# Attention row maxima over two PSUM banks at a time, with splits and sums moved to other engines

## The reference

```
b, s, d = x.shape                                   # 4, 512, 128; NH = 16 heads, DH = 8
qkv = x @ W_qkv.T + b_qkv
q, k, v = parts of qkv.reshape(b, s, 16, 24)
scores = einsum('bqhd,bkhd->bhqk', q, k) / sqrt(8)
attn = softmax(scores, axis=-1)
out = einsum('bhqk,bkhd->bqhd', attn, v).reshape(b, s, d)
return out @ W_out.T + b_out

x = x + 0.5 * ffn(layernorm(x))
x = x + attention(layernorm(x))
x = x + 0.5 * ffn(layernorm(x))
```

## Time and profile before

| | us |
|---|---|
| median of three runs | 1564.73 |
| the profiled execution | 1565.24 |
| its span | 1563.5 |
| attention steps alone on the chip | 708.8 to 902.4 of the span |
| PE busy | 1474.1 |
| DVE busy | 1308.9 |
| ACT busy | 1209.7 |
| POOL busy | 976.3 |

### The profile page before, as it was taken

One profiled execution on the slowest core, in us unless ns is written; L12 is line 12 of the kernel. 1 busy time (PEld: TensorE's weight loads), 2 busy tenths in 40 slices (PEclk: granted clock), 3 DMA queues, 4 the chain that ended last, 5 costly groups with the idle time before them and its releaser, 6 DMA issues. The chain is left out here.

```text
span 1563.5 us, 25918 instructions
## 1 busy us (share of the span) xinstructions
PE 1474.1 (94%) x7227; PEld 1101.0 (70%) x7227; DVE 1308.9 (84%) x3532; ACT 1209.7 (77%) x3587; POOL 976.3 (62%) x1719
## 2 busy tenths in 40 slices
PE   4898999999999999978988899999999999999997
PEld 3577778888888888743333347888888888888884
DVE  6989889988998877868898948988898889887884
ACT  3677888888888888737886687888888888888884
POOL 3477887777777776642332125777677767776665
PEclk8899999999999999979998999999999999999999
DMA  6144433333343235301211012233233233333321
GB/s 196 41 162 148 162 135 109 108 109 108 109 135 109 108 109 202 109 27 68 72 55 64 27 55 82 108 109 108 109 115 109 108 109 115 110 115 116 125 83 34
DMA packets 50838, 163.49 MB, mean 105 GB/s; under 512 B 3460, under 2 KB 26630, under 8 KB 34310
## 3 DMA queue, kind: packets, MB, share of 16 engines
q1 hardware_dynamic: 50694, 161.82, 29.8%
HBM read 136.64 MB, written 25.17 MB: 103 GB/s over the span
## 5 line engine op out<-in xcount | busy, mean ns | idle before, releaser
L989 ACT ACTIVATE vt<-bank,gate 128x128 f32<-128x128 f32 x1024 | 293.3, 372 | 169.1 <-PE bank L520 152.1
L1349 DVE SCALAR_TENSOR_TENSOR ot<-bank,gn,ot 128x128 f32<-128x128 f32 x1024 | 288.1, 344 | 82.7 <-ACT ot L1028 51.3
L1636 POOL TENSOR_TENSOR vt<-vt 128x256 f32<-128x256 f32 x256 | 193.7, 757 | 240.9 <-DVE vt L1335 240.7
L1028 ACT ACTIVATE ot<-bank,gn 128x128 f32<-128x128 f32 x1024 | 292.6, 371 | 41.9 <-PE bank L520 31.7
L1335 DVE SCALAR_TENSOR_TENSOR vt<-bank,gate,vt 128x128 f32<-128x128 f32 x1024 | 286.0, 342 | 12.3 <-ACT vt L989 10.6
L1661 POOL TENSOR_TENSOR ot<-ot 128x256 f32<-128x256 f32 x256 | 200.9, 785 | 100.2 <-DVE ot L1349 95.6
L1358 DVE TENSOR_TENSOR pt<-bank,pt 128x512 fp32r<-128x512 f32 x256 | 175.9, 687 | 74.9 <-ACT pt L1016 74.3
L518 PE MATMUL bank<-wv,xhl 128*128 128x512 f32 x512 | 225.8, 441 | 13.4 <-ACT vt L989 12.0
L518 PE MATMUL bank<-wo,chl 128*128 128x512 f32 x512 | 208.6, 407 | 21.8 <-DVE chl L1318 19.6
L1005 ACT ACTIVATE pp<-bank,nmin 128x512 f32<-128x512 f32 x256 | 180.5, 705 | 36.6 <-DVE nmin L1325 34.4
L1325 DVE TENSOR_REDUCE nmin<-bank 128x1 f32<-128x512 f32 x256 | 173.9, 679 | 39.8 <-PE bank L520 37.8
(11 more groups left out here) (192 smaller groups left out, 3039.8 us busy)
## 6 DMA issues: line engine op xcount, KB each, us to landing
wv<-wv_split SPq DMA_DIRECT2D x56, 1024.0 KB, 4.9
wo<-wo_split SPq DMA_DIRECT2D x56, 1024.0 KB, 4.8
wv_split<-wv SPq DMA_DIRECT2D x8, 1024.0 KB, 5.1
wo_split<-wo SPq DMA_DIRECT2D x8, 1024.0 KB, 7.1
qk<-qk_rows SPq DMA_DIRECT2D x32, 256.0 KB, 2.9
qk_rows<-qs SPq DMA_DIRECT2D x24, 256.0 KB, 3.0
rawv<-in_L_ffn_v_w SPq DMA_DIRECT2D x8, 512.0 KB, 6.8
rawo<-in_L_ffn_o_w SPq DMA_DIRECT2D x8, 512.0 KB, 8.8
```

The source lines that it names most:

```text
L989: last = activation(vt[:, u % 2, e * P:(e + 1) * P], gb[0][:, e * P:(e + 1) * P], ACT.Copy, scale=gate[:, n % 2, k, h * E + e:h * E + e + 1])
L1028: last = activation(ot[:, u % 2, e * D:(e + 1) * D], gb[2][:, e * D:(e + 1) * D], ACT.Copy, scale=gn[:, j % 2, k, e:e + 1])
L1349: last = v.scalar_tensor_tensor(o, gb[3][:, e * D:(e + 1) * D], gn[:, j % 2, k, G + e:G + e + 1], o, ALU.mult, ALU.add)
L1636: own.link(g_.tensor_tensor(a[:, 0:2 * P], a[:, 0:2 * P], a[:, 2 * P:4 * P], ALU.add))
```

## The change

- `pair[i]` is a PSUM tensor over two banks; the eight banks are its halves.
- PE computes the scores of two steps, s and s + 1, at even s. They take pair 0 (banks 0 and 1) for the first 6 steps, and then pair 0 and pair 2 (banks 4 and 5) in turns.
- DVE reduces the two banks in one instruction of 128 x 2 x 512 to two maxima.
- The small products have no bank of their own any more. They take their turn in the ring of the transposed scores (6, 2 and 3; bank 6 up to step 30; 2 and 3 from step 280).
- The split of the maxima moves from DVE to POOL, to the same step.
- The division by the sums is taken apart. After each group ACT copies the 8 results and the sum of each head (`copy_sums`, 128 x 144) to `oR`; once in a batch DVE takes the reciprocals of all 64 sums and POOL multiplies (128 x 512). The transposes that follow wait for this one product.

```diff
 def ring(what, s):
     if what == "attention":
-        return (0, 1) if s < EARLY else (4, 0, 1)
-    if what == "turned":
-        return 6, 2, 3
-    return (5,) if s < LAST_SMALL else (2,)
+        return (s % 2,) if s < EARLY else (s % 2, 4 + s % 2)
+    if s < LAG:
+        return (6,)
+    return (6, 2, 3) if s < LAST_SMALL else (2, 3)
...
+SUMS = MU - GU + TURN_OUT + 2
...
+        pair = [ctx.enter_context(nc.psum_tensor(f"pair{i}", [P, 2, 512], F32)) for i in range(4)]
+        bank = [pair[i // 2][:, i % 2, :] for i in range(8)]
...
 # PE
                 elif what == "out":
-                    pe.wait_ge(on_ready, i + 1)
+                    pe.wait_ge(out_copied, i + 1)
...
-                    if s < STEPS:
+                    if s < STEPS and s % 2 == 0:
                         score(s)
+                        score(s + 1)
                     if 0 <= i < STEPS:
                         score_t(i)
...
 # ACT
+                def copy_sums(G):
+                    b, g = G // NG, G % NG
+                    act.wait_ge(ott_mm, G + 1)
+                    if g == 0 and b >= 1:
+                        act.wait_ge(on_ready, b)
+                    o = place(("out", G))[:].rearrange("p (k j r) -> p k j r", k=QT, j=GH)
+                    activation(oR[:, :, GH * g:GH * g + GH, :], o[:, :, :, 0:DH + 1], ACT.Copy).then_inc(out_copied, 1)
...
 # DVE
                 def row_max(s):
-                    G = s // GU
-                    dve.wait_ge(ms_mm, s + 1)
+                    G, j = s // GU, s % GH
+                    dve.wait_ge(ms_mm, s + 2)
                     if s % GU == 0 and G >= 2:
                         dve.wait_ge(m_split, G - 1)
-                    v.tensor_reduce(mmax[:, G % 2, s // GH % QT, s % GH:s % GH + 1], place(("attention", s))[:],
-                                    AX.X, ALU.max).then_inc(m_max, 1)
+                    v.tensor_reduce(mmax[:, G % 2, s // GH % QT, j:j + 2], pair[PLACE[("attention", s)][0] // 2][:],
+                                    AX.X, ALU.max).then_inc(m_max, 2)
...
+                def over_sums(b):
+                    dve.wait_ge(out_copied, NG * (b + 1))
+                    if b >= 1:
+                        dve.wait_ge(on_ready, b)
+                    v.reciprocal(mrd[:], oR[:, :, :, DH]).then_inc(mrd_ready, 1)
...
 # POOL
+                def split_maxima(G):
+                    pool.wait_ge(m_max, GU * (G + 1))
+                    if G == 0:
+                        pool.wait_ge(mrow_set, 1)
+                    else:
+                        pool.wait_ge(m_tr, G)
+                    own.link(g_.tensor_copy(mrow[:, :, :, 3], mmax[:, G % 2, :, :]))
+                    g_.tensor_tensor(mrow[:, :, :, 7], mmax[:, G % 2, :, :], mrow[:, :, :, 3].bitcast(F32), ALU.subtract)\
+                        .then_inc(m_split, 1)
+
+                def over_sums(b):
+                    pool.wait_ge(mrd_ready, b + 1)
+                    if b >= 1:
+                        pool.wait_ge(ont_mm, b)
+                    g_.tensor_tensor(oN[:], oR[:, :, :, 0:DH], mrd[:].unsqueeze(3).to_broadcast([P, QT, NH, DH]), ALU.mult)\
+                        .then_inc(on_ready, 1)
...
+                    if batch_of(s - LAG, SUMS) is not None:
+                        over_sums(batch_of(s - LAG, SUMS))
+                    if group_of(s, GU - 1) is not None:
+                        split_maxima(group_of(s, GU - 1))
```

More of the change, by code:

```diff
@@ L263, in macaron_kernel @@
         wo_split = nc.dram_tensor("wo_split", [H, P, 2 * E * D], F32, kind="Internal").ap()
-        bank = [ctx.enter_context(nc.psum_tensor(f"bank{i}", [P, 512], F32)) for i in range(8)]
+        pair = [ctx.enter_context(nc.psum_tensor(f"pair{i}", [P, 2, 512], F32)) for i in range(4)]
+        bank = [pair[i // 2][:, i % 2, :] for i in range(8)]
         gb = bank[0:4]
@@ L1120, in step @@
                         copy_out(group_of(i, TURN_OUT - 2))
+                    if group_of(i, TURN_OUT + 1) is not None:
+                        copy_sums(group_of(i, TURN_OUT + 1))
                     if batch_of(s, PUT_VALUES + 1) is not None:
```

35 lines of the change are left out of this document (8 added, 27 removed).

## The result

The changed kernel takes 1592.34 us (median of 4 runs, 1578.40 to 1597.65), the kernel before beside it 1563.96 (4 runs, 1563.17 to 1564.85): a ratio of 1.0172, 95% interval 1.0143 to 1.0202. I had forecast 1548 and a range up to 1562. The profiled execution is one of the slower, 1597.65 us over a span of 1595.9, against 1565.24 and 1563.5. The four runs of the changed kernel differ in one more thing: their mean granted clock is 0.953, 0.963, 0.954 and 0.970 in the order 1597.65, 1587.16, 1597.51, 1578.40 us. The lower the clock, the longer the run. The profile of before has 0.976.

What follows compares the result with a forecast made beforehand. DVE was taken as the bound, with PE carrying its delay. Gains of 2.1 + 6.8 + 6.5 + 2 us in four attention stretches, less 0.5 after the last score, made 16.9: 1565.2 to 1548 us, range 1536 to 1562.

Steps and rivals of the forecast that it cites:

- The reduction over two banks: DVE's row maxima: one reduction of 1024 columns takes 1.15 us against 1.257 for two, saving 0.053 us a step.
- Splits and sums leave DVE: DVE in the attention steps: loses 0.069 us a step, gains 0.009 for a reciprocal, net 0.060 saved.
- DVE has the most work per step and is the bound: Middle attention stretch: DVE, busy 88.58 of 100 us, sets the pace, with PE as the carrier of its delay.
- the pace falls to ACT's 0.70: Middle attention stretch: the fullest engine goes from 0.732 to 0.70 us a step, ACT being the fullest.
- my 0.77: Middle attention stretch: 0.07 over ACT's 0.70 gives 0.77 us a step instead of 0.826, saving 6.8 us.
- Banks, costed at a few tenths of ACT's idle time and nothing for PE: Small products in the transposed scores' banks: larger ones leave ACT idle a few tenths; PE's waits on the small bank go.
- the shared banks eat it: Rival, chance 0.18: PE stands at small products until an exponential is done; step stays near 0.82, 1562 us.
- The tail, costed at 0.5 us: After the last score: nothing gained, and two more ACT copies cost 0.5 us.
- The split on POOL: Moved split of the maxima: about 0.5 us of work, due seven steps later, 5 us of cover; costed at nothing.
- Before the first exponential, 2 us: 30 steps beside the first feed-forward pass's end: two pairs remove most PE waits for row maxima; 2 us (0 to 4).
- The rival of the clock: Rival, chance 0.10: longer PE pauses bring 130 more steps at half clock, +30 - 17 = +13, 1578 us.
- The sign of a late split: Sign that the forecast is wrong: POOL's splits become what the maxima's transposes wait for.

Runs made afterwards that it cites:

- i_filler: Changed kernel with one extra 128x128x512 matmul before every second score from step 30 on, overwritten by it; 1599.55 us, 1.0234 of before.
- a_moved_work: Kernel before with only splits and sums moved off DVE; banks and single row maxima as before; 1563.71 us, 1.0010 of before.
- e_short_max: Kernel before with row maxima over the first 128 of 512 columns; 1538.35 us, 0.9843 of before.
- q_old_tail: Changed kernel going back to the banks of before after the last step's scores; 1586.82 us, 1.0132 of before.
- r_order: Changed kernel with POOL's split of the maxima queued behind input_rest instead of ahead at steps 31, 95 and 159; 1574.94 us, 1.0078 of before.
- s_early_order: Kernel before with four score banks in the first 30 steps, splits and sums off DVE, POOL's split queued behind input_rest; 1557.81 us, 0.9968 of before.
- c: Kernel before with only banks changed: single scores from four banks, small products in the transposed scores' ring; 1572.25 us, 1.0049 of before.
- h: Kernel before with four score banks and small products in bank 6 for the first 30 steps only; 1557.64 us, 0.9965 of before.
- run 51: Not a run label: 51 counts the additional steps at the low clock level in the changed kernel's profiled execution, which took 1597.65 us.

## Why the prediction was wrong, point by point

- **The reduction over two banks**: right in kind, slightly off in size. 1218 ns, not 1150, against 1257 for two streamed ones: 0.02 us a step saved, not 0.053. Not a cause.
- **Splits and sums leave DVE**: the work left as counted. The copy of the sums cost ACT 305 ns each (forecast 390), the split's copy 214 and its subtraction 236 on POOL (240 each), the product 1.08 us (1.28).
- **"DVE has the most work per step and is the bound", and the pace falls to ACT's 0.70**: this is the step that failed first. I read PE's 88.91 of 100 us as "not work at full rate" and left PE out of the search for the next bound. i_filler shows 0.73 us a step of PE's work at full clock, as much as DVE's 0.732. a_moved_work took 0.06 us a step from DVE and got nothing (0.003); e_short_max took 0.40 and got 0.065, to 0.755 with PE busy 93.65 of 100. So my 0.77 asked PE to run nearly without a pause, in a kernel that gave it new waits.
- **Banks, costed at a few tenths of ACT's idle time and nothing for PE**: failed second. The rings alone cost 9 us (1.0049); the rival *the shared banks eat it* had this mechanism, PE at the oldest bank until an exponential is done, but gave it only the power to cancel a gain: 1562. The tail, costed at 0.5 us, took 6.0, and q_old_tail shows it is the ring.
- **The split on POOL, "I cost it at nothing"**: failed third, 9 to 17 us by r_order, though only in company of the pairs and the shared ring (a_moved_work, s_early_order). I looked at the split's reader (seven steps away, right) and named two pieces of work queued behind it; the one that mattered, `input_rest`, I did not name, and it waited for nothing of DVE's before.
- **Before the first exponential, 2 us**: 5.6. Right in mechanism; the banks alone bring it (c, h: 45.8 and 45.4 against 50.0), not DVE's relief (a: 48.9).
- **The rival of the clock** had the right sign and much of the size: 1578 for 130 steps more at the low level. In the profiled run 51 were enough, since the gain it should first have eaten did not exist and a low step costs 0.46, not 0.23, more. Its sign came true: the granted clock of the stretch alone is 0.79, well below 0.93. The sign of a late split did not: POOL waits for DVE with it, but the transposes of the maxima (L801) show no wait for POOL. My chance of 0.10 for the clock rested on a faster pace with the same matmuls, so that PE pauses less. The pace did not rise, and PE's pauses stayed what they were in sum: idle 10.4 us of the 100 from 740 to 840 us, 11.1 before.

The Trainium skill, "TensorE: Matmul & The Clock Gate", section on PSUM-queue depth-cycling, warned that a PE pausing between groups while it cycles its banks can swing between levels. In the prediction I let the middle stretch speak against it. The trace after agrees with the warning in that the clock fell, to 0.96 there and 0.51 behind it. That pauses between groups brought it about is not shown: in the middle PE is idle no more than before, and in the long spell it is shown idle for 2.2 of 66 us.

**What stays open.** Why the clock stays low for 65 us at one time and not at another of the same kernel (0.953 to 0.970 over the four runs); why the split costs with pairs and shared rings and not without, and how much of its 9 to 17 us is stall and how much clock; and whether the pace of s, 0.784, would pay if the clock held. The parts add up only roughly: rings +9, pairs +3.5, split +10.7 and sums -3.3 make 20, and the whole is 28 in the first measurement of the changed kernel and 20 in the second, and the pairs' and the sums' parts are within the noise.

## What to carry to other kernels

Before crediting relief of the fullest engine, ask whose queue sets the pace: an experiment that shortens that engine's work alone (here a maximum over a quarter of the columns) gives the ceiling, and a filler on the next engine shows how much pause it has left. When an instruction with a new wait is put on another engine's in-order queue, list everything behind it down to the next product that PE waits for, and put it behind that. Widen a ring only while its extra banks are otherwise unused. And profile a kernel twice before reading a spell of low clock or a small difference in pace as its own.

## What the runs showed of the hardware that I had not expected

- Less work on TensorE can cost time. With three quarters of the columns of one of its three large products gone, it was granted 0.5 for 188.8 of 209.8 us, the low steps took 0.939 us each, and the kernel became 1.4% longer.
- TensorE stayed at 0.5 while its records show it busy 63.82 of 66 us, so a full row of PE in the profile is no assurance of the higher level. The fall came right after a stretch with long pauses, at the four reciprocals of DVE; here 852 to 856 and then 860 to 864 us, after:

```profile
852.00:856.00 4.00, 2.58 (x24) 0.82 (x16) 4.00 (x5) 2.62 (x5) 0.00 (x0) 1.00 0.41 131
...
860.00:864.00 4.00, 4.00 (x20) 1.71 (x12) 3.12 (x5) 1.71 (x4) 0.00 (x0) 0.50 0.00 0
```

- One reduction over two banks saves only 0.04 us against two that stream (1218 ns against 1257).
